# Recommendation tower: a first table in halves, four lookups ahead of the second pair, transposes and MLP steps in another order

## What is computed

```python
e = stack([tbl_f[ids[:, f]] for f in range(26)], axis=1)          # 2048 x 26 x 128
sd = einsum('bfd,bd->bf', e, dense)                               # 26 products with the dense vector
ss = einsum('bfd,bgd->bfg', e, e); pairs = ss[:, iu, ju]          # 325 products of features with each other
z = concatenate([dense, sd, pairs], axis=1)                       # 479 numbers
h = maximum(concatenate([z, dense], axis=1) @ W_top1 + b_top1, 0) # 607 -> 512
h = maximum(h @ W_top2 + b_top2, 0)                               # 512 -> 256
y = h @ W_top3                                                    # 256 -> 1
```

## Time and profile before

| | us |
|---|---|
| median of 3 runs | 361.55 (360.44 to 361.70) |
| the profiled execution's own time | 359.05 |
| its span from first to last instruction | 357.1 |

### The profile page before, as it was taken

The page is one execution under the profiler, slowest core; times in us unless marked ns, Lnnn a source line. Parts: engine busy times, 40 slices in busy tenths (PEclk is TensorE's granted clock), DMA queues, the critical chain, the costliest instruction groups (busy, mean ns, idle before and its releaser), DMA issues.

```text
span 357.1 us, 8260 instructions
## 1 busy us (share of the span) xinstructions
PE 335.2 (94%) x3388; PEld 286.4 (80%) x3388; DVE 206.6 (58%) x486; ACT 204.0 (57%) x267; POOL 241.8 (68%) x242
## 2 busy tenths in 40 slices
PE   0799999697999999999999999999999999999996
PEld 0677777586988888888998888898898888898885
DVE  0889898565328874628328886527427787145111
ACT  3378897484736575763663664872572666664111
POOL 6777777777777777777777777777777777720000
PEclk9999999999999999999999999999999999999999
DMA  6999729536355225254247243246236321124400
GB/s 154 241 261 250 194 61 269 148 93 164 76 143 138 65 69 132 55 127 124 53 108 183 75 105 84 68 95 155 59 83 177 100 64 48 51 51 121 113 24 1
DMA packets 46342, 40.93 MB, mean 115 GB/s; under 512 B 29039, under 2 KB 40423, under 8 KB 46306
## 3 DMA queue, kind: packets, MB, share of 16 engines
q1 hardware_dynamic: 38754, 24.94, 27.4%
q0 software_dynamic: 7552, 15.48, 17.3%
HBM read 34.64 MB, written 5.76 MB: 113 GB/s over the span
## 4 chain that ended last, share of the span: by engine, by line
PE 77%; POOL 8%; DMA 5%; issue 4%; DVE 3%; SPq 2%; ACT 1%; DVEq 0%
PE oh_ps L538 34%; PE dot_ps L556 15%; PE mlp_ps L574 15%; POOL rows L367 8%; PE mlp_ps L583 7%; PE tr_ps L522 7%; DMA rows<-tbl_dram,idx_sb 3%; DVE onehot L462 2%; DMA b_sb<-b_top_dram 2%; ACT feat L391 1%; DMA idx_sb<-idx_dram 0%; SPq L320 0%; SPq L316 0%; SPq L319 0%; DVE h L481 0%
## 5 line engine op out<-in xcount | busy, mean ns | idle before, releaser
L367 POOL DMA_INDIRECT rows<-tbl_dram,idx_sb x236 | 241.3, 1023 | 73.3 <-issue 70.7
L462 DVE TENSOR_SCALAR onehot<-ids_bc 125x512 fp32r<-125x512 int16 x360 | 142.4, 448 | 33.2 <-PE oh_ps L538 19.1
L538 PE MATMUL oh_ps<-onehot,table_hi 125*128 125x512 f32 x360 | 115.5, 402 | 12.0 <-DVE onehot L462 11.9
L538 PE MATMUL oh_ps<-onehot,table_lo 125*128 125x512 f32 x360 | 111.7, 392 | 0.0
L399 ACT ACTIVATE feat<-oh_ps 128x512 f32<-128x512 f32 x45 | 54.7, 1217 | 62.8 <-PE oh_ps L538 61.7
L391 ACT ACTIVATE feat<-tr_ps 128x512 f32<-128x512 f32 x59 | 73.0, 1241 | 26.3 <-PE tr_ps L522 25.8
L538 PEld LDWEIGHTS oh_ps<-onehot,table_hi 125*128 125x128 f32 x360 | 65.6, 190 | 24.4 <-issue 12.8
L538 PEld LDWEIGHTS oh_ps<-onehot,table_lo 125*128 125x128 f32 x360 | 68.1, 189 | 14.8
L556 PE MATMUL dot_ps<-feat 128*54 128x52 f32 x2048 | 57.8, 214 | 5.7 <-ACT feat L391 1.8
L556 PEld LDWEIGHTS dot_ps<-feat 128*54 128x54 f32 x2048 | 54.5, 130 | 10.1 <-issue 6.1
L471 DVE COPY dots<-dot_ps 54x416 f32<-54x416 f32 x56 | 33.2, 594 | 36.2 <-PE dot_ps L556 34.9
(11 more groups left out here) (24 smaller groups left out, 65.4 us busy)
## 6 DMA issues: line engine op xcount, KB each, us to landing
ids_bc<-ids_t_dram SPq DMA_DIRECT2D x45, 128.0 KB, 3.9
dots_scratch<-dots SPq DMA_DIRECT2D x28, 175.5 KB
rows<-tbl_dram,idx_sb POOLq DMA_INDIRECT x236
dots<-tbl_dram SPq DMA_DIRECT2D x6, 480.0 KB
w_sb<-tbl_dram SPq DMA_DIRECT2D x3, 480.0 KB
zt<-dots_scratch SPq DMA_DIRECT2D x12, 117.0 KB
dense_sb<-dense_f_dram SPq DMA_DIRECT2D x8, 128.0 KB, 2.6
zt<-tbl_dram SPq DMA_DIRECT2D x2, 480.0 KB
```

What stands on the lines that cost most here:

```text
L367: nc.gpsimd.indirect_dma_start(rows[:, i % RING, k, t, :], None, tables[f], bass.IndirectOffsetOnAxis(ap=idx_sb[:, j % 2, x:x + 1], axis=0 ...
L462: last = nc.vector.tensor_scalar(onehot_part(m, part)[:, c, :], ids_bc[0:TP, m % IDSLOTS, :], float(part * PROWS + c), None, ALU.is_equal)
L538: last = nc.tensor.matmul(oh_ps[:, m % 2, :], table[0:TP, u, row * D:(row + 1) * D], onehot_part(m, part)[:, c, :], start=(table is table_ ...
```

## The change

1. The first table is loaded ahead of any ids, in two halves of 512 columns; ScalarE and VectorE split each half as it comes (`a0`, `b0`), and the first lookup starts on the first half. ScalarE's queue issues the first ids. The ids lie in DRAM once for each partition instead of being broadcast from one row.
2. TensorE begins with 24 transposes of the identity matrix.
3. VectorE waits for the MLP weights after the dot products of chunk 0 instead of before them.
4. Lookups 2 and 3 of pair 1 (numbers 14 and 15, `EXTRA`) write `mlp_ps`, and four lookups stand ahead of the dot products of chunk 1. The first layer-1 step then waits until ScalarE has copied both of them out.
5. In all lists transposes stand later: `r9` of pair 0 behind its last lookup, `q13` and `q14` of pairs 1 and 3, `q14` of pair 2 in the list that follows. In the tail, `k3` and `k4` stand ahead of the dot products of the last chunk.
6. The last chunk's products are stored by SyncE and ScalarE, two DMAs each, and layer 3 of chunk 5 stands ahead of the last copies.

```diff
-FIRST = ("i0 s0 i1 s1 l0 c0 i2 s2 l1 c1 i3 s3 r0 l2 c2 i4 s4 r1 l3 c3 i5 s5 r2 l4 c4 s6 i6 r3 l5 c5 s7 i7 r4 "
-         "l6 c6 s8 i8 r5 l7 c7 s9 i9 r6 f l8 c8 s10 i10 l9 c9 s11 i11 r8 l10 c10 r9 j0 l11 c11 e0 e1 e2 e3 r10 j1 "
-         "e4 e5 g j2 e6 e7 r11 j3 j4 j5")
-SECOND = ("l0 q12 l1 q13 q14 d0 d1 d2 d3 d4 d5 d6 c0 d7 c1 o0 r0 o1 o2 r1 o3 r2 o4 "
...
-         "j0 m0 g m1 e0 e1 r11 e2 e3 e4 e5 e6 e7 r12 m2 j1 m3 r13 j2 j3 m4 r14 j4 j5")
-LEAD = "l0 l1 r0 o0 o1 r1 d0 d1 d2 d3 d4 d5 d6 c0 d7 c1 r2 o2 r3 o3 o4 r4 "
...
-TAIL = "k2 d0 d1 d2 d3 d4 d5 d6 d7 k3 k4 o0 o1 o2 o3 o4 m0 m1 m2 m3 m4"
+EXTRA = (LOOKUPS[0] + 2, LOOKUPS[0] + 3)
+HALF = RPP * D // 2
+WARM = 24
+FIRST = ("i0 a0 b0 i1 s1 l0 c0 i2 s2 l1 c1 i3 s3 r0 l2 c2 i4 s4 r1 l3 c3 i5 s5 r2 l4 c4 s6 i6 r3 l5 c5 s7 i7 r4 "
+         "l6 c6 s8 i8 r5 l7 c7 s9 i9 r6 f l8 c8 s10 i10 l9 c9 s11 i11 r8 l10 c10 j0 l11 c11 r9 e0 e1 e2 e3 r10 j1 "
+         "e4 e5 g j2 e6 e7 r11 j3 j4 j5")
+SECOND = ("l0 q12 l1 q13 l2 l3 q14 d0 d1 d2 d3 d4 d5 d6 c0 d7 c1 c2 c3 r0 o0 o1 o2 r1 o3 r2 o4 i6 "
+         "l4 c4 r3 i7 l5 c5 r4 i8 l6 c6 r5 l7 c7 i9 l8 c8 r6 i10 f l9 c9 r7 l10 c10 r8 "
+         "j0 m0 g m1 e0 e1 e2 e3 r9 e4 e5 e6 e7 r10 m2 j1 m3 j2 r11 m4 j3 r12 j4 j5")
+THIRD = ("l0 l1 q13 o0 o1 q14 d0 d1 d2 d3 d4 d5 d6 c0 d7 c1 r0 o2 o3 r1 o4 r2 "
...
+         "j0 m0 g m1 e0 e1 r10 e2 e3 e4 e5 e6 e7 r11 m2 j1 r12 m3 j2 j3 m4 r13 j4 j5")
+LAST = ("l0 l1 q14 o0 o1 r0 d0 d1 d2 d3 d4 d5 d6 c0 d7 c1 r1 o2 o3 r2 o4 r3 "
...
+        "m0 m1 e0 e1 e2 e3 r11 e4 e5 e6 e7 r12")
+TAIL = "k2 k3 q13 k4 q14 d0 d1 d2 d3 d4 d5 d6 d7 o0 o1 o2 o3 o4 m0 m1 m2 m3 m4"
```

```diff
+        def lookup_out(m):
+            if m in EXTRA:
+                return mlp_ps[:, EXTRA.index(m), :]
+            return oh_ps[:, m % 2, :]
...
+            def load_first_table():
+                raw = raw_table(0)
+                src = tables[ONEHOT[0]].rearrange("(r c) d -> r (c d)", c=RPP)
+                for half in range(2):
+                    cs = slice(half * HALF, (half + 1) * HALF)
+                    loaded = table_loaded[0] if half else half_loaded
+                    sp.dma_start(raw[0:120, cs], src[0:120, cs]).then_inc(loaded, DMA)
+                    sp.dma_start(raw[120:TP, cs], src[120:TP, cs]).then_inc(loaded, DMA)
...
+                for q in range(Q if n < NCH - 1 else Q // 2):
+                    store_quarter(sp, n, q)
...
+            act.dma_start(ids_bc[:, 0, :], ids_t[0]).then_inc(ids_loaded[0], DMA)
...
+                    if kind == "d" and n == NCH and x == GUNITS - 1:
+                        act.wait_ge(dots_out_act, GUNITS * NCH)
+                        act.wait_ge(dots_out_dve, GUNITS * NCH)
+                        for q in range(Q // 2, Q):
+                            store_quarter(act, NCH - 1, q)
...
-            dve.wait_ge(weights_loaded, WEIGHT_DMAS * DMA)
-            nc.vector.tensor_tensor(w1_sb[:, ZC, :], w1_sb[:, ZC, :], w1_dense2, ALU.add).then_inc(w1_summed, 1)
...
+                lead = PARTS * (4 if j == 1 else 2)
                 if j:
-                    for i in range(PLACES, 2 * PARTS + PLACES):
+                    for i in range(PLACES, lead + PLACES):
                         make_part(looked(j) + i // PARTS, i % PARTS)
                     dots_to_sbuf(n - 1)
                     layer3(n - 2)
...
                 dots_to_sbuf(n)
-                if 0 < j < NPAIR - 1:
+                if j == 0:
+                    dve.wait_ge(weights_loaded, WEIGHT_DMAS * DMA)
+                    nc.vector.tensor_tensor(w1_sb[:, ZC, :], w1_sb[:, ZC, :], w1_dense2, ALU.add
+                                            ).then_inc(w1_summed, 1)
+                elif j < NPAIR - 1:
                     layer3(n - 1)
+            layer3(NCH - 3)
             dots_to_sbuf(NCH - 1)
-            for n in range(NCH - 3, NCH):
+            for n in range(NCH - 2, NCH):
                 layer3(n)
...
+                if m in EXTRA:
+                    pe.wait_ge(warmed, 1)
+                elif m >= 2:
+
+                    pe.wait_ge(looked_up_out, m - 1 - 2 * (m - 2 in EXTRA))
...
                     if n == 0:
                         pe.wait_ge(weights_loaded, WEIGHT_DMAS * DMA)
                         pe.wait_ge(w1_summed, 1)
+                        pe.wait_ge(looked_up_out, EXTRA[-1] + 1)
...
+            pe.wait_ge(ident_made, 1)
+            for i in range(WARM):
+                last = nc.tensor.transpose(mlp_ps[:, i % 2, 0:P], ident[:], ident[:])
+            last.then_inc(warmed, 1)
```

More of the change, by code:

```diff
@@ L86, in looked, with has_odd @@
     return sum(LOOKUPS[:j])
+def has_odd(j):
+    return LOOKUPS[j] == NO
 def unit_no(j, u):
-    return UNITS * j - (j > 0) + u - (j == 0 and u > ALONE)
+    return UNITS * j - sum(not has_odd(i) for i in range(j)) + u - (not has_odd(j) and u > ALONE)
 def pair(row):
@@ L238, in dot_copy, with store_quarter @@
             return dst, src
+        def store_quarter(engine, n, q):
+            products = dots_dram[n % 2, 0:NI * NJ, :].rearrange("(i j) b -> i j b", j=NJ)
+            row = TILE * (q // PACK) + NI * (q % PACK)
+            own = dots_of(n)[row:row + NI].rearrange("p (k j g) -> p k j g", k=PACK, j=NJ)
+            engine.dma_start(products[:, :, q * QS:(q + 1) * QS], own[:, q % PACK]
+                             ).then_inc(last_stored if n == NCH - 1 else dots_stored, DMA)
         block = ctx.enter_context(nc.Block())
@@ L274, in store_products @@
                 sp.wait_ge(dots_out_dve, GUNITS * (n + 1))
-                products = dots_dram[n % 2, 0:NI * NJ, :].rearrange("(i j) b -> i j b", j=NJ)
-                for q in range(Q):
-                    row = TILE * (q // PACK) + NI * (q % PACK)
-                    own = dots_of(n)[row:row + NI].rearrange("p (k j g) -> p k j g", k=PACK, j=NJ)
-                    sp.dma_start(products[:, :, q * QS:(q + 1) * QS], own[:, q % PACK]).then_inc(dots_stored, DMA)
+                for q in range(Q if n < NCH - 1 else Q // 2):
+                    store_quarter(sp, n, q)
             def make_z(n):
@@ L298, in _ @@
             load_idx(0)
-            for u in range(IDSLOTS):
+            load_first_table()
+            for u in range(1, IDSLOTS):
                 load_ids(u)
@@ L330, in _ @@
                     make_z(n - 1)
-                    for u in range(NO - 2, NO):
+                    for u in range(NO - 2, LOOKUPS[j]):
                         load_ids(looked(j) + u)
@@ L355, in _ @@
             for j, u in itertools.product(range(NPAIR), range(UNITS)):
[L356 removed]
+                if u == ALONE and not has_odd(j):
                     continue
@@ L483, in layer3 @@
                                                    ).then_inc(y_made, 1)
-            for u in range(NO + 1):
+            make_part(0, 0)
+            split_first_lo(0)
+            make_part(0, 1)
+            split_first_lo(1)
+            make_part(0, 2)
+            make_part(0, 3)
+            for u in range(1, NO + 1):
                 split_lo(u)
@@ L537, in lookup @@
                             row = part * PROWS + c
-                            last = nc.tensor.matmul(oh_ps[:, m % 2, :], table[0:TP, u, row * D:(row + 1) * D],
+                            last = nc.tensor.matmul(lookup_out(m), table[0:TP, u, row * D:(row + 1) * D],
                                                     onehot_part(m, part)[:, c, :],
```

51 lines of the change are left out of this document (36 added, 15 removed).

## The result

| | before | after |
|---|---|---|
| median, us | 361.62 (360.44 to 362.36, 4 runs) | 368.77 (367.81 to 369.71, 4 runs) |
| ratio | 1 | 1.0201, 95% interval 1.0159 to 1.0243 |
| profiled execution, us | 359.05 | 369.71 |
| its span, us | 357.1 | 367.9 |

The change costs 7.15 us in the medians. Some executions of a kernel are over 1.5% slower than its fastest; medians and ratios leave them out.

What follows compares the result with a forecast made beforehand. TensorE's own list was taken to bound the kernel, with GpSimd's gathers setting a floor of about 352 us. The terms summed to +4.6, a span of 361.7 and a time of 366.1 us (ratio 1.013); range 359.3 to 368.3.

Steps and rivals of the forecast that it cites:

- Early start, 0: First pair: the first lookup starts some 3.3 us earlier, but the gain is waited away at late gathered rows; 0 us.
- `r9`, -0.65: End of pair 0: transposes moved behind the last lookup remove a 0.27 us wait and hide 0.44 us; -0.65 us.
- `q14` alone, -0.5: Before chunk 1's dot products: one copy to wait for instead of two, 1.3 us instead of 1.84; -0.5 us.
- Weights, -1.8: Chunk 0's dot products: TensorE's 1.77 us wait for VectorE, which stood at the MLP weights, goes; -1.8 us.
- Four lookups ahead, +4.1: Before the first layer-1 step: TensorE waits until ScalarE has copied two more lookups; +4.1 us.
- The clock in that gap: Rival, chance 0.15: the clock falls in the idle time before the first layer-1 step; 1.4 us more, +6.0, 367.5 us.
- `q14` ahead of `d0` twice, +2.6: Pair 2 and the tail: one copy must end before the dot products, 1.3 us each time; +2.6 us.
- The tail, +1.1: Last chunk: less work covers the products' store and reload, though two stores on ScalarE save 2.4 us; +1.1 us.
- the wait at 160.69: TensorE's 0.25 us wait for gathered rows at 160.69 us goes; -0.25 us.
- The faster rival: Rival, chance 0.13: the whole first pair runs at TensorE's pace from its first lookup; -2.9, 358.7 us.
- the rival of earlier rows: Rival, chance 0.12: rows of `r4` and `r5` come earlier and 3.0 us of early start survive; +1.6, 363.1 us.
- The rival of smaller waits: Rival, chance 0.10: the wait before `o0` costs half and the tail's wait is hidden; +1.5, 363.0 us.

## Why the prediction was wrong

The direction and the two largest waits were right in kind; two terms of the sum were too small, the clock behind the gap, put at nothing, and the tail. +4.6 was forecast, +7.15 measured, and 368.77 lies 0.5 above the range, with two of the four runs inside it. The terms, between the two profiled executions:

- **Early start, 0**: right in its size and in the reason, rows that land when they land, but not in its course. The second table landed earlier than forecast (its split began at 9.64, not 11.29) and its lookup started at 12.8, not 14.4. TensorE then waited for the rows of `r1`, `r2` and `r3`, not at `r4` and `r5`, and VectorE's 4.3 us a table did not bind. With the old beginning `r5` is done at about the same time. TensorE was 1.0 late at `r5`, while the term had bounds on the side of a gain alone: the rows landed at 43.55, and the low clock behind the wait at `r3` took 1.5 us of its own. That `r5` came out so near its old place is in part luck, and it lies within the spread between runs (42.2 to 43.6).
- **`r9`, -0.65; `q14` alone, -0.5**: between `r5` and the first dot products the changed kernel makes up 0.63 (from 0.99 behind to 0.36), and the wait there is 1.27 instead of 1.84. Both right.
- **Weights, -1.8**: right, 1.9 by the run of this part alone.
- **Four lookups ahead, +4.1**: 4.26 of wait in the trace. Right in the wait, but the term left out what stands behind it.
- **The clock in that gap**: the step that failed. It was put with the rivals, at a chance of 0.15, on the ground that 1.84 us of idle time had cost nothing. That was the wrong neighbour for 4.1 us: the steps took 1.9 us more than the sum had for them (5.2 to 7.05), 1.7 of it by the clock (5.35 with the wait filled), and the run with the wait filled gives 2.6 in the median.
- **`q14` ahead of `d0` twice, +2.6**: 1.27 and 1.27. Right.
- **The tail, +1.1**: mis-sized, the other step that failed. The saving of 2.4 by the second queue isn't there: the stores land 8.4 us after the last dot product with one queue or two. What ends last is their transfer, not their issue; the reload landed 2.0 after the end of its last issue, where 2.3 were estimated. So the wait was 2.3, above the upper bound of 1.8, and the steps behind it took another 1.8 (6.92 to 8.72), most of it by the clock: behind the same wait at full clock they take 7.19 in the run with the lookup in the gap. The prediction had this cost for the other gap alone. ScalarE's two stores also held up the ReLU, so that the work that covers the reload took 0.6 more (11.0 instead of 10.4).

Added up over the traces: 1.0 - 0.6 - 1.8 - 0.6 + 4.3 + 1.9 + 2.5 + 2.3 + 1.8 and 0.6 for the ReLU behind ScalarE's stores, -0.3 for the wait at 160.69, is 11.1, against 10.8 between the spans. In the medians the difference is 7.15. Part of the rest is that the profiled run of before was 2.6 faster than its median; the trace of the kernel before with only the weights moved has 1.4 us of low clock that the trace of before has not, and 2.5 us of waits for rows where that has 1.2, which shows that such losses come and go from run to run. How much of the 3.5 each of them makes was not measured.

The faster rival, a first pair at TensorE's pace, and the rival of earlier rows did not come about: `r5` held. The rival of smaller waits was wrong on both of its waits.

## What to carry to other kernels

Before an engine's steps are placed earlier, look for what its next step needs from another engine's ordered list: here a two-copy longer queue on ScalarE stopped all of TensorE, and one lookup moved into the gap gave back 5.9 us in the median, 5.2 of it in the gap by the trace. An early start is worth nothing ahead of a transfer that keeps its landing time; follow it to the next such landing before counting it. Idle time of the matmul engine is priced twice where it is long, once for itself and once for the clock behind it, so waits that can't be removed should be filled, and a second queue helps only where the issue, and not the transfer, ends last.

## What the runs showed of the hardware

- The 24 transposes of the identity, from 1.47 us on, lift the clock: in all seven traces outside the first chip that have them the first lookup goes at the full pace (0.46 us for two matmuls), against 0.85 for two in the three without them. It brings nothing to this kernel, since the time is lost again at the rows, and in three of the seven the clock fell again behind the wait of the second lookup (1.93, 1.94 and 2.62 us).
- The clock falls not by the longest gap alone. 2.3 us of idle time at `r3` brought it down in the changed kernel (granted clock 0.72 from 33 to 39 us) but not in the run with the lookup in the gap, which waited 2.28 us there and has a mean granted clock of 1.00. Behind single waits of 1.9 to 2.6 us it fell in 10 of 18 cases of these traces, behind 1.94 us in one and not behind 2.55 in another; what else decides was not found. Behind the 4.26 us gap it fell in all four traces that have it unfilled, and the three layer-1 steps took 7.05, 7.11, 7.11 and 8.05 us against 5.35 at the full clock.
- Gathers issued while tables fill the DMA engines land 7.2 to 8.6 us after they start (35.41 to 43.54 for the last one of `r5` in the changed kernel, 29.82 to 38.45 for that of `r4` in the run with one queue), against 3.5 in the quiet part, though the gathers themselves are still issued every 1.3 to 1.5 us.
